# Edge lists of a graph layer: two negated copies made after the first pair of one-hot tables, and a two-column square on ScalarE while the lists are made

## The reference

```python
xn = layernorm(x)
x = x + gnn(xn, W, a, src, dst) + linear_attention(xn, w_qkv, w_out, b_out)
x = x + moe(layernorm(x), router_w, rg, ru, rd, sg, su, sd)
# gnn: h = xn @ W; al = h @ a_l; ar = h @ a_r
# e = exp(-leaky_relu(al[src] + ar[dst])); rowsum = segment_sum(e, src)
# h' = segment_sum(e[:, None] * h[dst], src) / (rowsum + eps); elu(h')
```

## Time and profile before

| what | value |
|---|---|
| median of 3 runs | 2824.89 us (2823.66 to 2825.5) |
| span of the profiled execution | 2825.1 us |
| TensorE busy | 2804.8 us (99%) |
| VectorE busy | 2233.2 us (79%) |
| ScalarE busy | 1489.3 us (53%) |
| GpSimd busy | 55.4 us (2%) |
| HBM traffic | 193 GB/s over the span |

### The profile page before, as it was taken

The page is one execution under the profiler, slowest core; times in us unless marked ns, Lnnn a source line. Parts: engine busy times, 40 slices in busy tenths (PEclk is TensorE's granted clock), DMA queues, the critical chain, the costliest instruction groups (busy, mean ns, idle before and its releaser), DMA issues.

```text
span 2825.1 us, 40627 instructions
## 1 busy us (share of the span) xinstructions
PE 2804.8 (99%) x14886; PEld 2317.9 (82%) x14886; DVE 2233.2 (79%) x2735; ACT 1489.3 (53%) x1941; POOL 55.4 (2%) x73
## 2 busy tenths in 40 slices
PE   9999999999999999999999999999999999999999
PEld 8975898788888888888888888888888888888877
DVE  8847256988888888888888888888888888888888
ACT  7722233555555555555555555555555555555563
POOL 0010000000000000000000000000000000000001
PEclk9999999999999999999999999999999999999999
DMA  4020131766666666666666666666666666666676
GB/s 114 15 83 30 60 105 45 228 217 223 223 236 223 217 212 234 222 217 214 218 214 213 215 226 211 218 216 229 219 216 216 225 219 219 224 223 217 220 263 233
DMA packets 270275, 549.06 MB, mean 194 GB/s; under 512 B 16673, under 2 KB 82465, under 8 KB 269927
## 3 DMA queue, kind: packets, MB, share of 16 engines
q1 hardware_dynamic: 265954, 532.11, 55.8%
q0 software_dynamic: 3936, 14.06, 1.6%
q10 hardware_dynamic: 162, 0.08, 0.0%
HBM read 537.49 MB, written 8.70 MB: 193 GB/s over the span
## 4 chain that ended last, share of the span: by engine, by line
PE 95%; DVE 3%; issue 0%; DMA 0%; ACT 0%; POOL 0%; POOLq 0%; DVEq 0%; SPq 0%; ACTq 0%
PE ps L1892 26%; PE ps L1896 26%; PE ps L1895 26%; PE ps L1660 3%; PE ps L1697 2%; PE ps L1699 2%; PE ps L1698 2%; PE ps L1750 2%; PE ps L1943 1%; PE ps L1784 1%; PE ps L1782 1%; PE ps L1783 1%; DVE C L990 0%; DVE c_lo L1087 0%; PE ps L1792 0%
## 5 line engine op out<-in xcount | busy, mean ns | idle before, releaser
L1439 DVE TENSOR_TENSOR c_lo<-raw,c_hi 128x1024 fp32r<-128x1024 f32 x832 | 985.1, 1219 | 99.8 <-ACT c_hi L809 99.4
L809 ACT CAST c_hi<-raw 128x1024 fp32r<-128x1024 f32 x832 | 862.9, 1050 | 157.1 <-PE ps L1896 156.7
L1892 PE MATMUL ps<-tok_hi,c_hi 128*128 128x314 f32 x1792 | 552.9, 309 | 2.8 <-DVEq L1627 1.7
L1896 PE MATMUL ps<-tok_hi,c_lo 128*128 128x314 f32 x1792 | 552.0, 308 | 0.0
L1895 PE MATMUL ps<-tok_lo,c_hi 128*128 128x314 f32 x1792 | 551.8, 308 | 0.0
L1892 PE MATMUL ps<-c_hi,xgT_hi 128*97 128x512 f32 x1024 | 404.6, 395 | 0.0
L1896 PE MATMUL ps<-c_hi,xgT_lo 128*97 128x512 f32 x1024 | 404.1, 395 | 0.0
L1895 PE MATMUL ps<-c_lo,xgT_hi 128*97 128x512 f32 x1024 | 403.3, 394 | 0.0
L1505 DVE TENSOR_TENSOR resid<-ps,resid 125x512 f32<-125x512 f32 x320 | 218.9, 686 | 178.4 <-PE ps L1896 178.2
L1892 PEld LDWEIGHTS ps<-tok_hi,c_hi 128*128 128x128 f32 x1792 | 339.4, 189 | 5.7 <-issue 1.8
L1895 PEld LDWEIGHTS ps<-tok_lo,c_hi 128*128 128x128 f32 x1792 | 339.8, 190 | 1.4
(11 more groups left out here) (251 smaller groups left out, 3526.2 us busy)
## 6 DMA issues: line engine op xcount, KB each, us to landing
raw<-in_L_ffn_rg SPq DMA_DIRECT2D x256, 512.0 KB, 4.8
raw<-in_L_ffn_ru SPq DMA_DIRECT2D x256, 512.0 KB, 4.7
raw<-in_L_ffn_rd SPq DMA_DIRECT2D x256, 512.0 KB, 6.2
raw<-in_L_ffn_sg SPq DMA_DIRECT2D x64, 512.0 KB, 5.4
raw<-in_L_ffn_su SPq DMA_DIRECT2D x64, 512.0 KB, 5.5
raw<-in_L_ffn_sd SPq DMA_DIRECT2D x64, 512.0 KB, 5.7
wl<-in_L_mix_w_qkv SPq DMA_DIRECT2D x6, 2048.0 KB, 7.9
wl<-in_L_gnn_W SPq DMA_DIRECT2D x2, 2048.0 KB, 23.1
```

The source lines that it names most:

```text
L809: nc.scalar.copy(c_hi[u % RING][:], raw_at_(q, r)[:]).then_inc(sem("hi_done"), 1 + (U - UNITS) * (u == UNITS - 1))
L1439: V.tensor_tensor(c_lo[u % RING][:], raw_at_(q, r)[:], c_hi[u % RING][:].bitcast(F32), ALU.subtract).then_inc(sem("lo_done"), 1 + (U - UNI ...
L1892: m = MM(out_, l_hi, r_hi, start=first, stop=False, skip_group_check=skip)
L1896: return MM(out_, l_lo, r_hi, start=False, stop=last, skip_group_check=skip)
```

## The change

The two negated copies are taken out of the row of seven and made by a function `negated`, which `between` calls after chunk 0 of group 0, that is after the first `oh_d` and `oh_s`. On ScalarE, after the second load is issued, the wait for `iota_done` comes first, then a square of two columns of `iota_h` into a scratch tile, and a wait for it; then come the waits for `indices` and `idx` and the tables as before.

```diff
@@ ScalarE
         act.dma_start(dst_i[0:REST, EC:ECP], dst[P * EC:NE].rearrange("(p c) -> p c", p=REST)).then_inc(sem("dst_in"), 16)
+        act.wait_ge(sem("iota_done"), 1)
+        nc.scalar.activation(sq_s[1][:, 0:2], iota_h[:, 0:2], ACT.Square).then_inc(sem("squares"), 1)
+        act.wait_ge(sem("squares"), 1)
         act.wait_ge(sem("indices"), 1)
         act.wait_ge(sem("idx"), 6)
-        act.wait_ge(sem("iota_done"), 1)
         for gr in range(NG):
@@ VectorE
         V.tensor_scalar(dig_f[:], odd_i[:], HIGH - LOW, LOW, ALU.mult, ALU.add).then_inc(sem("idx"), 1)
-        V.tensor_scalar(src_n[:], half_i[:], -1.0, None, ALU.mult).then_inc(sem("idx"), 1)
-        V.tensor_scalar(dig_n[:], odd_i[:], LOW - HIGH, -LOW, ALU.mult, ALU.add).then_inc(sem("indices"), 1)
         dve.wait_ge(sem("iota_done"), 1)
         dve.wait_ge(sem("idx"), 5)
+
+        def negated():
+            V.tensor_scalar(src_n[:], half_i[:], -1.0, None, ALU.mult).then_inc(sem("idx"), 1)
+            V.tensor_scalar(dig_n[:], odd_i[:], LOW - HIGH, -LOW, ALU.mult, ALU.add).then_inc(sem("indices"), 1)
@@ VectorE, what is called between tables
-        between = [{}] + [{9: lambda g=gr - 1: add_digits(g, 0), 13: lambda g=gr - 1: add_digits(g, 1)}
+        between = [{0: negated}] + [{9: lambda g=gr - 1: add_digits(g, 0), 13: lambda g=gr - 1: add_digits(g, 1)}
                           for gr in range(1, NG)]
```

## The result

The changed kernel is slower: 2829.38 us, median of 16 runs (2827.18 to 2830.99), against 2823.93 us for the kernel before, 16 runs beside it (2822.85 to 2826.49). The two ranges do not touch. The ratio is 1.0018, its 95% interval 1.001 to 1.0025; the difference of the medians is 5.45 us. Forecast were 2824.7 us and a range that ended at 2827.1.

The account below looks back on a forecast made before the run. TensorE was taken to carry the chain, with everything before its first matmul serial. Moved copies gave -0.17 us, square and table load 0, so the median 2824.89 became 2824.7 us; range 2822.3 to 2827.1.

Parts of the forecast that it names:

- the sentence on the two-column square: ScalarE before the indices arrive: one added instruction and two waits, hidden while ScalarE stands idle, cost 0.
- The copies' move: VectorE at the start: first `oh_d` starts at 4.54 instead of 4.71 us, first matmul 0.17 us earlier.
- Rival C: VectorE at the start: the first `oh_d` does not come forward, the change does nothing, 2824.9 us; chance 0.15.
- The second pair: VectorE's second `oh_d` and `oh_s`: end 0.12 us later, at 6.22, still hidden from TensorE with 0.51 us to spare.
- The table load off ScalarE's path: ScalarE at the start: 1.28 us of function table load leave its path, worth nothing to the end.
- Whether the 0.1 us reaches the end: Whole kernel: the gain at the first matmul, forecast as 0.17 us, moves everything behind it along to the end.
- The slow beginning of TensorE: TensorE's first matmuls, until 10.04 us: 0.26 us spacing, then 0.13; gain 0.085 us if that moment stays, 0.17 if it follows.
- Rivals A and B: Clock: one slow piece less, 2822.9 us, chance 0.13; or one more between 470 and 490 us, 2826.5, chance 0.11.
- anything of another size: Anywhere, such as a second table load inside the loops, 32 quarters at 1.28 us, 41 us; chance 0.04, both sides.
- the 0.2% that I had called no change: Whole kernel time: a measurement tells some 0.2%, 5.6 us, from no change; within that, chance 0.96.

Follow-up runs that it names:

- the place +3: Loop three instructions further on through reached waits: changed kernel with two more instructions, 2823.93 us; moved copies alone with three, 2822.91 and 2823.24; kernel before with three, 2823.31.

## Why the prediction was wrong

**The step that failed** is the sentence on the two-column square: "It adds one instruction (and two waits) ... so all of it lies in a stretch in which ScalarE stands anyway." The sum has no term for it. Its time does lie there, 0.20 us at 3.24. But I priced it by the time alone, and the instruction also takes a place in ScalarE's program. That moved everything behind it, the loop over the experts among it, by one, across a boundary of the pieces in which the program is brought in. Cost: 5.45 and 4.66 us in the two measurements of the changed kernel, 3.76 for the square and its waits alone and 4.69 for one wait without work, against the 0 that I gave it. That the turns matter at all could have been asked of the trace of before: its wait of 0.9 us for `c_lo` and the second casts that come after 1.08 to 2.67 us instead of 0.34 at just five of the steps were there, and I had not looked at ScalarE's loop since the change was so far from it.

**What held.** The copies' move came forward: `oh_d` starts 0.34 to 0.37 us behind the start of `dig_f` in the nine traces with the move, and 0.46 in the four without it, so 0.10 us and not 0.17. The term was too large because the wait for `dig_f` costs more than the 0.02 to 0.06 us that I took from other rows: 0.12 us from its end at 4.15 to 4.27 in the changed kernel. The trace of before was a poor base besides: its first `oh_d` takes 0.50 us and `oh_s` follows 0.43 behind it, in the twelve other traces 0.38 or 0.39 and 0.30. Rival C of the prediction, that nothing comes forward, is out. The second pair stayed hidden. The table load off ScalarE's path was worth nothing, as forecast: the kernels with and without it at the place +3 have the same stretch, and their medians, each against the kernel before beside it, lie within 0.5 us (-0.77 with it, -0.88 to -1.25 without).

**Whether the 0.1 us reaches the end** can't be seen. The slow beginning of TensorE does not end a fixed time after the first matmul: that matmul started at 4.98 to 5.54 us in the traces read, and the fast spacing began anywhere from 8.3 to 10.8 us, in the kernel before at 10.04 after 17 slow matmuls, in the changed kernel at 10.79 after 22 and in its second trace after 17. The rule of the Trainium skill (TensorE: Matmul & The Clock Gate, Part 1) that I had set beside the term, that the count of slow matmuls differs from run to run, is borne out by these two traces of one program. Rivals A and B, one clock piece less or more, describe what single executions do, but not what moved the medians.

**The chances.** I gave 0.04 to anything of another size, with the example of a second table load in the loops. The measured change, 0.19% by the medians and 0.18% by the ratio, is inside the 0.2% that I had called no change, and still clear of it: 16 runs on each side tell more than I granted.

## What to carry to other kernels

An instruction added to an engine whose program loops later is not free merely because the engine is idle where it stands: count the instructions ahead of the loop on that engine and look at its turns in the trace (the first instructions behind the turn against the same ones in an ordinary step). If a turn is late, a few waits that are already reached, put where the engine stands anyway, move the loop's head to a better place; here two more instructions were worth 5 to 6 us against the changed kernel. And compare profiles by stretches that the clock leaves alone, not by two spans.

## What the runs showed of the hardware that I had not expected

ScalarE's instructions come in transfers of 8192 bytes, by the packets behind its branches, and the pattern repeats after 128 instructions; where the boundary lies close behind the loop's head, the first cast behind a turn is 2.0 to 3.5 us late (4.23 to 5.73 instead of 2.20). A profile may put such a gap down to TensorE or to "issue". Why the second packet starts only 4.0 to 6.0 us behind the branch, why TensorE's single wait behind such a turn is anything from 0.4 to 1.2 us, and why the moved copies alone lost only 0.17 us in their stretch (1304.84) where the kernel before lost 1.71 at the same place, stays open: one trace of each stands against the other, and I have not repeated them.
